# Cross-attention and a routed expert layer: the turned probabilities of the second half of the heads in a PSUM bank of their own, with new bank tenants and new instruction orders

## What is computed

```python
x = x + jnp.tanh(g_xattn[0]) * attention(_layernorm(x), ctx_1024, ctx_1024, Wq, Wk, Wv, Wp, bp)
x = x + jnp.tanh(g_ffn[0]) * experts(_layernorm(x), gate_kernel, w0_kernel, w1_kernel, wo_kernel)
# attention: kp, vp = rope(k @ Wk.T), rope(v @ Wv.T); softmax(q k / sqrt(8)) v per head; @ Wp.T + bp
# experts: the two largest of the 8 gate logits, softmax over the two,
#          (silu(x w0[e]) * (x w1[e])) wo[e], weighted and summed
```

## Time and profile before

| | us |
|---|---|
| median of 3 runs | 672.11 (670.93 to 673.26) |
| the profiled execution | 671.08 |
| its span, first to last instruction | 669.3 |
| TensorE, VectorE, ScalarE, GpSimd busy | 579.3, 399.4, 422.1, 374.7 |
| mean granted TensorE clock | 0.96 of full speed |

### The profile page before, as it was taken

The page is one execution under the profiler, slowest core; times in us unless marked ns, Lnnn a source line. Parts: engine busy times, 40 slices in busy tenths (PEclk is TensorE's granted clock), DMA queues, the critical chain, the costliest instruction groups (busy, mean ns, idle before and its releaser), DMA issues.

```text
span 669.3 us, 20945 instructions
## 1 busy us (share of the span) xinstructions
PE 579.3 (87%) x6121; PEld 480.9 (72%) x6122; DVE 399.4 (60%) x1354; ACT 422.1 (63%) x1098; POOL 374.7 (56%) x516
## 2 busy tenths in 40 slices
PE   8999989999999999999989897886879878888870
PEld 6887767767776777777777696675668778778770
DVE  4788777777777777777879552271222322323573
ACT  2788777777777777778878664352545455565550
POOL 3135656656566565665656566575555555455561
PEclk8999999999999999999999987997989999999895
DMA  2811212112121121211212212223322222225887
GB/s 75 238 51 43 68 54 67 47 43 71 47 63 51 51 63 47 67 48 57 63 49 63 78 57 67 73 89 95 97 73 74 76 73 77 65 74 176 259 268 220
DMA packets 72946, 57.18 MB, mean 85 GB/s; under 512 B 9119, under 2 KB 68768, under 8 KB 72880
## 3 DMA queue, kind: packets, MB, share of 16 engines
q1 hardware_dynamic: 55552, 35.05, 18.4%
q0 software_dynamic: 8448, 16.93, 7.7%
q10 hardware_dynamic: 8880, 4.39, 2.3%
HBM read 29.44 MB, written 23.22 MB: 79 GB/s over the span
## 4 chain that ended last, share of the span: by engine, by line
PE 59%; another core or an unknown queue 12%; issue 8%; ACT 7%; DVE 5%; ACTq 3%; DMA 2%; POOL 2%; DVEq 1%; SPq 1%; POOLq 0%
PE psG L558 11%; PE psH L491 9%; PE psH L477 7%; PE psH L600 7%; PE psH L483 5%; PE psK L502 3%; ACT wcur L758 3%; PE psO L533 2%; ACTq L320 2%; PE psG L616 2%; PE psO L616 2%; PE psG L505 2%; PE psO L522 2%; ACT ys L772 2%
## 5 line engine op out<-in xcount | busy, mean ns | idle before, releaser
L1236 POOL DMA_INDIRECT results<-ys,zin x136 | 135.8, 998 | 105.5 <-ACT ys L772 66.1
L1173 POOL DMA_INDIRECT lists<-zp,dest x128 | 129.7, 1013 | 46.8 <-issue 35.7
L600 PE MATMUL psH<-zT,wcur 128*128 128x128 f32 (+1 forms) x760 | 138.3, 332 | 17.3 <-ACT wcur L758 13.1
L600 PEld LDWEIGHTS psH<-zT,wcur 128*128 128x128 f32 x760 | 113.6, 197 | 30.6 <-ACT wcur L758 17.6
L695 ACT ACTIVATE ex<-psH,rs 128x512 f32<-128x512 f32 x128 | 81.2, 684 | 70.0 <-PE psH L483 58.2
L1076 DVE TENSOR_TENSOR hm<-psH,hs 128x512 f32<-128x512 f32 x68 | 47.0, 691 | 129.8 <-PE psH L600 39.1
L968 DVE TENSOR_REDUCE mx<-psH 128x8 fp32r<-128x512 f32 x128 | 83.9, 684 | 18.7 <-PE psH L477 14.2
L558 PEld LDWEIGHTS psG<-v,pT 128*64 128x64 f32 x2048 | 66.9, 138 | 30.5 <-issue 30.5
L699 ACT COPY pT<-psH 128x512 f32<-128x512 f32 x128 | 76.1, 595 | 15.2 <-PE psH L491 11.9
L558 PE MATMUL psG<-v,pT 128*64 128x64 f32 x2048 | 77.9, 225 | 4.1 <-issue 3.7
L491 PE MATMUL psH<-ident,ex 128*128 128x128 f32 x512 | 78.8, 278 | 0.5 <-ACT ex L695 0.5
(11 more groups left out here) (165 smaller groups left out, 1039.2 us busy)
## 6 DMA issues: line engine op xcount, KB each, us to landing
yy<-results SPq DMA_DIRECT2D x16, 512.0 KB
zin<-lists SPq DMA_DIRECT2D x41, 130.0 KB
xres<-x1r SPq DMA_DIRECT2D x32, 128.0 KB
out_dram<-xres ACTq DMA_DIRECT2D x16, 256.0 KB
xring<-in_x_dram SPq DMA_DIRECT2D x31, 128.0 KB
cring<-in_ctx_dram SPq DMA_DIRECT2D x31, 128.0 KB
zin<-lists SPq DMA_DIRECT2D x54, 65.0 KB
results<-ys,zin POOLq DMA_INDIRECT x136
```

The lines of the kernel that those rows point to most:

```text
L600: last = pe.matmul(bank[t.buf(2)][:, k * ET + c.start:k * ET + c.stop], wcur[:, t.buf(2), h, a, k * P:(k + 1) * P], zT[:, t.buf(2), c], st ...
L1173: nc.gpsimd.indirect_dma_start(lists, bass.IndirectOffsetOnAxis(ap=dest[:, t.buf(4), j:j + 1], axis=0), zp[:, t.buf(4), j, :], None).then_ ...
L1236: nc.gpsimd.indirect_dma_start(results, bass.IndirectOffsetOnAxis(ap=zin[:, t.buf(8), h, D:D + 1].bitcast(U32), axis=0), ys[:, t.buf(8), h ...
```

## The change

1. `turn(t, 1)` writes the second half's turned probabilities side by side into psG; the first half's still go to psH[0]. The scores of the second half now wait for the exponentials of the tile before instead of the copy.
2. The other tenants move: PV from psG to the right half of psK, turned `on` from psG to psO, the places from psG to psX; the experts' banks are dealt out anew too.
3. New orders. TensorE's step now begins with rows turned, shift of the first half, output product, shift of the second half, turned keys, keys and values; then `on`, the first half's probabilities, the second half's, queries, scores, PV. Output product, keys and values and maxima are for other tiles than before (one step later or earlier). DVE begins with `rden` and `on` and ends with the maxima of the first half, then of the second. ACT begins with `xcT` and takes the first half first. POOL begins with `kvr`, then `ve` and `rs`, then both scatters in a row.
4. At the end of the stage some expert work is put into attention steps elsewhere, and the scatters end one step earlier.

The core of the diff:

```diff
-ATT_PE = Pipeline(NT, behind=1, ahead=5, unroll=8, steady=5, turns=5)
-ATT_DVE = Pipeline(NT, behind=2, ahead=6, unroll=8, steady=7, turns=5)
-ATT_ACT = Pipeline(NT, behind=7, ahead=1, unroll=8, steady=12, turns=5)
-ATT_POOL = Pipeline(NT, behind=6, ahead=5, unroll=8, steady=11, turns=5)
+ATT_PE = Pipeline(NT, behind=2, ahead=5, unroll=8, steady=6, turns=5)
+ATT_DVE = Pipeline(NT, behind=2, ahead=5, unroll=8, steady=7, turns=5)
+ATT_ACT = Pipeline(NT, behind=6, ahead=1, unroll=8, steady=11, turns=5)
+ATT_POOL = Pipeline(NT, behind=5, ahead=5, unroll=8, steady=10, turns=5)
...
-        psA, psB = [psH[0][:, 0, :], psH[0][:, 1, :]], [psH[1][:, 0, :], psH[1][:, 1, :]]
-        psZ, psY = [psX, psK], [psO, psG]
+        psA, psB = [psH[1][:, 0, :], psH[0][:, 0, :]], [psH[1][:, 1, :], psH[0][:, 1, :]]
+        psZ, psY = [psX, psG], [psK, psO]
...
+                def keys_values(t):
+                    wait_for(pe, xc_sb, t)
+                    wait_for(pe, rope_done, t, back=1)
+                    wait_for(pe, on_done, t, back=4)
+                    pe.matmul(psK[:, 0:2 * D], xcT[:, t.buf(8), P:2 * P], wT[:, 1:3, :], start=True, stop=True).then_inc(kv_ps, 1)
+
+                def queries(t):
+                    wait_for(pe, xc_sb, t)
+                    wait_for(pe, oT_sb, t, back=3)
+                    pe.matmul(psO[:, 0:P], wT[:, 0, :], xcT[:, t.buf(8), 0:P], start=True, stop=True).then_inc(q_ps, 1)
...
-                            last = pe.transpose(psH[h][:, n // 2, o:o + P], ex[:, t.buf(2), h, n * P:(n + 1) * P], ident[:, :])
+                            into = psG[:, n * P:(n + 1) * P] if h else psH[0][:, n // 2, o:o + P]
+                            last = pe.transpose(into, ex[:, t.buf(2), h, n * P:(n + 1) * P], ident[:, :])
                         last.then_inc(p_ps[h], 1)
...
+                    if t := ATT_PE.at(s, 5):
+                        inputs_turned(t)
...
+                        wait_for(pe, mx_done[0], t)
+                        shift(0)
+                    if t := ATT_PE.at(s, 0):
+                        wait_for(pe, oT_sb, t)
                         pe.matmul(psO[:, 368:368 + XW], xcT[:, t.buf(8), 0:P], idg[:, :], start=True, stop=False, skip_group_check=True)
                         pe.matmul(psO[:, 368:368 + XW], oT[:, t.buf(2), :], wTg[:, :], start=False, stop=True, skip_group_check=True).then_inc(attn_ps, 1)
+                    if t := ATT_PE.at(s, 2):
+                        wait_for(pe, mx_done[1], t)
+                        shift(1)
...
+                        if u := ATT_PE.at(s, 5):
+                            wait_for(pe, xc_sb, u)
+                        wait_for(pe, kvr_done, t)
+                        pe.transpose(psX[:, 256:384], kvr[:, t.buf(2), 0:D], ident[:, :]).then_inc(kT_ps, 1)
...
+                    if t := ATT_PE.at(s, 5):
+                        keys_values(t)
+                    if t := ATT_PE.at(s, 1):
+                        wait_for(pe, on_done, t)
+                        wait_for(pe, x1_done, t, back=1)
+                        pe.transpose(psO[:, P:2 * P], on[:, t.buf(2), :], ident[:, :]).then_inc(oT_ps, 1)
+                    if t := ATT_PE.at(s, 2):
+                        wait_for(pe, exp_done[0], t)
+                        turn(t, 0)
+                    if (t := ATT_PE.at(s, -2)) and t.buf(4) == 3:
+                        if u := ATT_PE.at(s, 3):
+                            wait_for(pe, k_sb, u)
+                        places(t, psX)
...
+                    if t := ATT_PE.at(s, 2):
+                        wait_for(pe, exp_done[1], t)
+                        wait_for(pe, p_sb[1], t, back=1)
+                        turn(t, 1)
+                    if (t := ATT_PE.at(s, 4)) and not static(s, -4):
+                        queries(t)
+                    if t := ATT_PE.at(s, 3):
+                        if static(s, -3):
+                            pe.wait_ge(wT_sb, 2)
+                        wait_for(pe, k_sb, t)
+                        wait_for(pe, q_sb, t)
+                        wait_for(pe, exp_done[1], t, back=1)
+                        scores(t, 1)
...
+                        wait_for(pe, v9_done, t)
                         if u := ATT_PE.at(s, 5):
+                            wait_for(pe, rope_done, u)
+                        wait_for(pe, p_sb[0], t)
+                        wait_for(pe, p_sb[1], t)
+                        for n in range(PAIRS):
+                            for b in range(2):
+                                o = n % 4 * P + b * S
+                                last = pe.matmul(psK[b * S:(b + 1) * S, 2 * D + n * VW:2 * D + n * VW + VPAD], pT[:, t.buf(2), n // 4, o:o + S],
+                                                 v9[:, t.buf(4), b, n * VW:n * VW + VPAD], start=True, stop=True)
+                        last.then_inc(pv_ps, 1)
...
                     def probabilities(t, h):
-                        nc.scalar.copy(pT[:, t.buf(2), h, :].rearrange("p (g c) -> p g c", g=2),
-                                       psH[h][:, :, 256:512]).then_inc(p_sb[h], 1)
...
+                        if h:
+                            nc.scalar.copy(pT[:, t.buf(2), 1, :], psG[:, :]).then_inc(p_sb[1], 1)
+                        else:
+                            nc.scalar.copy(pT[:, t.buf(2), 0, :].rearrange("p (g c) -> p g c", g=2),
+                                           psH[0][:, :, 256:512]).then_inc(p_sb[0], 1)
...
-                    if t := ATT_DVE.at(s, 2):
-                        wait_for(dve, s_ps[1], t)
-                        wait_for(dve, shift_ps[1], t, back=1)
-                        maxima(1)
-                    if t := ATT_DVE.at(s, 2):
-                        wait_for(dve, s_ps[0], t)
-                        wait_for(dve, shift_ps[0], t, back=1)
-                        maxima(0)
...
+                    if t := ATT_DVE.at(s, 1):
+                        wait_for(dve, pv_ps, t)
+                        wait_for(dve, oT_ps, t, back=2)
+                        o = psK[:, 2 * D:2 * D + PAIRS * VW].rearrange("p (h w) -> p h w", w=DH + 1)
+                        nc.vector.reciprocal(rden[:, :], o[:, :, DH]).then_inc(rden_done, 1)
...
+                    if t := ATT_DVE.at(s, 3):
+                        wait_for(dve, s_ps[0], t)
+                        wait_for(dve, shift_ps[0], t, back=1)
+                        maxima(0)
+                    if t := ATT_DVE.at(s, 3):
+                        wait_for(dve, s_ps[1], t)
+                        wait_for(dve, shift_ps[1], t, back=1)
+                        maxima(1)
...
-                    if t := ATT_POOL.at(s, -6):
-                        scatter(t, (0,))
...
-                    if t := ATT_POOL.at(s, -6):
-                        scatter(t, (1,))
...
+                def attention_step(s):
+                    if t := ATT_POOL.at(s, 4):
+                        wait_for(pool, rope_done, t)
+                        wait_for(pool, kT_ps, t, back=2)
+                        wait_for(pool, v9_done, t, back=2)
+                        nc.gpsimd.tensor_tensor(kvr[:, t.buf(2), :], ropA[:, t.buf(2), :], ropB[:, t.buf(2), :],
+                                                ALU.add).then_inc(kvr_done, 1)
+                    if (t := ATT_POOL.at(s, -2)) and t.buf(4) == 3:
+                        tokens(t)
+                    if not static(s, NT - 1):
+                        powers(ATT_POOL.at(s, 0), ATT_POOL.at(s, 3))
+                    if (t := ATT_POOL.at(s, -2)) and t.buf(4) == 3:
+                        counted(t)
+                    if t := ATT_POOL.at(s, -5):
+                        scatter(t, range(2))
+                    if static(s, NT):
+                        powers(ATT_POOL.at(s, -1), None)
+                    if (t := ATT_POOL.at(s, -1)) and t.buf(4) == 3:
+                        wait_for(pool, chosen_done, t)
+                        for i in range(3):
+                            wait_for(pool, before_done, t, back=4 - i)
+                            nc.gpsimd.tensor_tensor(before[:, i + 1, :], before[:, i, :], chosen[:, i, :], ALU.add).then_inc(before_done, 1)
...
-                    if t := ATT_POOL.at(s, 4):
-                        wait_for(pool, rope_done, t)
...
                 pool.wait_ge(zero_ready, 3)
-                ATT_POOL.run(pool, attention_step, until=NT + 1)
+                ATT_POOL.run(pool, attention_step, until=NT)
```

334 lines of the change are left out of this document (134 added, 200 removed).

## The result

The kernel after takes **673.49 us** in the median (671.15 to 677.55, 20 runs) against 671.57 (668.51 to 673.77, 20 runs) of the kernel before on the same chip: a ratio of 1.0042, 95% interval 1.0025 to 1.0058. It was forecast at 655 us. The profiled execution has a span of 669.4 us, that of before 669.3.

The account below looks back on a forecast made before the run. It took TensorE, busy 87% of the span, as the bound, with scatters lengthening attention steps. 56 x (5.97 - 5.66) = -17.4 us, -1 + 1, seam 0: 671.1 to 653.7, plus 1.0 for the median, about 655 us; range 636 to 682.

Parts of the forecast that it names:

- (a): Attention steps: scatter pairs fall on tight hand-overs, slower; 680 us if half the steps, 708 if all; 20%.
- (b): Attention steps: no change, the loss belongs to the scatter whatever stands around it; 672 us within 2; 11%.
- part 3: POOL's new order: scatter pairs delay TensorE's signals, 0.25 us lost a scatter; with TensorE's stop, step 5.66 us.
- Part 1: Work in each attention step: the same matmuls and copies, sum 0; the undisturbed step stays at 5.03 us.
- Part 2: Slack of hand-overs in TensorE's order: first half's shift to turned probabilities 0.25 to 0.64 us; PV to `on` still 0.6.
- The step of 4.98 us: Attention step of before right after one of 6.6 us, said to have no scatter inside; used as evidence against (b).
- Part 4: The rest: `chosen` -1 us, the places +1, seam to the experts between -5 and +5, taken as 0.
- the places' matmuls: Every fourth attention step they wait for the keys' mask in psX: 0 to 0.3 us x 14, taken as 1 us.
- what `chosen` gave: DVE's `chosen`, moved away from POOL's `kvr`: -1 us taken of a possible 0 to -7.6.
- (c): Attention steps: most of the scatter loss goes; step 5.3 us, -37 us, 634 us; 14%.
- The sign: Whole kernel: faster, by -17.4 us; chances 0.67 faster, 0.10 within 0.3%, 0.23 slower.

Follow-up runs that it names:

- before_plain: Kernel before with GpSimd's indirect transfers for tiles 0 to 47 replaced by SyncE's plain ones and fixed routing: 564.78 us on a free chip, one run.
- after_again: Kernel after, unchanged, on a free chip: 551.43 us against 567.33 of the kernel before, ratio 0.9711.
- on_turned_in_psH_3: Kernel after with `on` turned into psH[1] instead of psO, queries waiting for x1r: 680.50 us on a holding chip, one run, before at 665.30.

## Why the prediction was wrong

It said 655 us because the step beside the scatters would fall from 5.97 to 5.66 us; measured it is 5.95. The 673.5 us lie inside the stated range of 636 to 682 only because the rivals (a) and (b) widened it; the forecast's own 643 to 668 missed. **The step that failed is part 3: the loss of 0.25 us a scatter, which was 0.56.** By the parts:

- *Part 1, the undisturbed step stays at 5.03 us.* Wrong, in the kernel's favour: 4.79 to 4.83. The step of the argument that failed is "TensorE is busy all the time (35.20 of 35.20 us)": I took a busy engine for a working one. 0.19 us of the scores' 0.87 were a wait. Part 2 even had it in hand ("scores wait for the copies of both halves", "hardly 0.1 us of slack for the first half") and priced it at nothing. On free chips this term is most of the result: 50 x (5.09 - 4.86) + 7 x 0.2 = 12.9 of 15.9 us, if the step of before is there that of before_plain. The last six steps go the other way (5.88 us against 4.98 of before_plain).
- *Part 2, slack.* For the exponentials it was right: their idle time fell from 70.0 to 31.7 us. For `on` the text found another 0.6 us and called the wait "not removed"; it is gone (1.1 us in all before L552 in after, 0.4 in after_again). What it left out is the one wait that the diff adds ahead of this matmul, for x1r in the same bank. In the undisturbed step L529 ends at 40.17 + 0.40 = 40.57, x1r takes 0.30, and L552 starts at 41.17: 0.3 us for two notices. That is about the slack of the second half's turning (0.26), and the list of hand-overs did not have it. It is where TensorE stood, but not why the time stayed: with this wait gone the step was no shorter (on_turned_in_psH_3).
- *Part 3, 0.25 us of loss a scatter.* This is the term that decided. Measured on the holding chip it is (5.95 - 4.83) / 2 = **0.56 us a scatter**, more than before's (5.95 - 5.03) / 2 = 0.46. Where the pairs fall was forecast well: 0.1, 1.4 and 3.6 us into TensorE's step, and in the disturbed step above, which begins with the turned rows at 208.66, it is -0.04, 1.35 and 3.24 (208.62, 210.01, 211.90). The price was built from three late hand-overs in two steps, 1.0 us together, and charged the first pair with the turned probabilities. In that step five other signals are late, by 1.0 to 1.6 us each: both shifts, the output product, the turned keys, and the keys and values. About two of three signals near a scatter are held, more of them over the second scatter of a pair than before; TensorE stands for the nearest consumer, and when that wait is taken away another stands there (on_turned_in_psH_3). The rivals (a), the pairs with a turning point of 0.47 us a scatter, and (b), "the loss belongs to the scatter, whatever stands around it", had the mechanism between them; (b) also had the time. It was given 11%. The step of 4.98 us that spoke against it is no argument: a step without a scatter inside loses nothing by (b) either, and this one in fact has one, from 223.62 us on, 0.5 us before its end.
- *Part 4.* Before the places' matmuls TensorE lost under 0.02 us a step; what `chosen` gave was not separated. Of the range, "most of (c)" is wrong by its own number: 634 us lies outside 636 to 682. The rest after the last `on` came out 1.0 us shorter, within the 5 us; the last six attention steps, where the experts begin, 3 us longer.
- *The sign.* 50 steps kept their 5.95 us, six lost 3 us, the first seven gained 1 and the rest 1. In the profiled executions that is a tie (669.3 and 669.4 us), in the medians a loss of 1.9 us, where the forecast had -17.4.

What the text could not know is that the 5.97 us went with the chip that it ran on. On a free chip the change gives 0.9711.

Open stays why the middle step came out so nearly equal in both kernels (5.95 and 5.95 us, and 5.91 and 5.88 in the later jobs), though their undisturbed steps differ by 0.2; and what holds the signals.

## What to carry to other kernels

A window in which the profile calls TensorE busy all the time may still hold waits: compare the time that equal groups of weight loads take, not the busy share, before a step is called bound by its work. For every wait that a diff adds, work out the slack even where it looks harmless, above all where two users are put into one PSUM bank. And if signals are late for a reason outside the order (here GpSimd's indirect transfers), do not sum the lateness by its present consumers: here moving one away only showed the next, and only taking away the source shortened the step. A verdict on such a kernel needs more than one chip.

## What the hardware showed

- On some chips TensorE's semaphore signals are held back beside GpSimd's indirect transfers: in the attention stage about two thirds of those within 1.6 us behind a transfer's start come over 0.3 us late (203 of 312 in after), none of those further away (479), and they can be noticed together (205.99 and 206.03 us for ends at 204.06 and 204.44). On free chips none of 455 is late (x1r 0.03 us after the product). The transfers last 1001 ns on both.
- Two such transfers 1.3 to 1.4 us apart can hold a signal over both, up to 2.8 us in after.
- Between the kinds of chip lie 97 to 104 us of 568 for the kernel before. The experts' stage has its part in it: from the last `on` to the end the kernel after takes 276.7 us on a holding chip and 219.0 on a free one. Signals are late there too (97 of 167 near a transfer in after, 7 of 267 in after_again), but no run took the transfers of that stage away, so it is not shown that all of the 58 us comes from them.
- Plain transfers of the same rows, issued by SyncE, hold nothing back (none of 725 signals late, steps of 4.91 us on a holding chip, in one run).
